# A transformer layer on one core: softmax sums from the blocks of maxima in place of a product with ones

## The reference

```
x = x + 0.5 * ffn(layernorm(x))      # ffn: weights rounded to -1, 0, 1 times their mean size, plus bias
x = x + attention(layernorm(x))
x = x + 0.5 * ffn(layernorm(x))

# attention: 16 heads of 32; b = 4, s = 1024
kqv = x @ Wqkv + bqkv
scores[k, q] = k_row . q_row / sqrt(32)     # kept where k <= q (triu), else -10000
attn = softmax(scores, over k)              # the kept ones of each q sum to 1
out = (attn^T @ v) @ Wo + bo
```

## Time and profile before

| | us |
|---|---|
| median of 3 runs | 1316.94 (1316.63 to 1317.14) |
| the profiled execution | 1315.88 |
| its span | 1313.7 |
| PE, DVE, ACT, POOL busy | 1235.4, 832.7, 501.9, 348.2 |
| L1079, the product with ones, PE | 160.3 |
| L747 and L741, maxima, DVE | 220.4 and 159.0 |
| L758, reciprocals, DVE | 118.9 |
| L897, exponentials, ACT | 314.6 |

### The profile page before, as it was taken

How to read it: one execution, slowest core, us unless ns; L and a number is a source line. 1 busy time by engine, 2 the same in 40 slices (tenths; PEclk the granted TensorE clock), 3 DMA queues, 4 the chain that set the end, 5 groups by cost and what they waited for, 6 DMA issues and landing times.

```text
span 1313.7 us, 27193 instructions
## 1 busy us (share of the span) xinstructions
PE 1235.4 (94%) x10938; PEld 749.1 (57%) x10938; DVE 832.7 (63%) x2048; ACT 501.9 (38%) x1139; POOL 348.2 (27%) x492
## 2 busy tenths in 40 slices
PE   4689999999999999999999999999999999998886
PEld 3466554555666565655656565655656566654454
DVE  6764556688545667689645767679644666655444
ACT  1222434344434334343433434344443434334421
POOL 4821110245001222236100322336201222300233
PEclk8898999999999999999999999999999999989988
DMA  7422201011103001321102102311102102000110
GB/s 240 145 81 80 83 34 59 26 63 44 42 2 130 18 34 49 114 82 49 50 1 99 49 10 74 113 66 58 41 18 73 58 26 74 26 10 10 42 49 32
DMA packets 40685, 77.26 MB, mean 59 GB/s; under 512 B 5232, under 2 KB 10352, under 8 KB 40560
## 3 DMA queue, kind: packets, MB, share of 16 engines
q1 hardware_dynamic: 40560, 75.52, 17.0%
HBM read 49.81 MB, written 25.17 MB: 57 GB/s over the span
## 4 chain that ended last, share of the span: by engine, by line
PE 84%; DVE 9%; issue 3%; POOL 2%; ACT 2%; DMA 1%; SPq 0%; DVEq 0%; ACTq 0%; POOLq 0%
PE bank L964 28%; PE bank L1024 11%; PE bank L1046 11%; PE bank L1068 10%; PE bank L1079 9%; PE bank L989 8%; PE bank L981 3%; PE bank L1052 3%; DVE mst L741 2%; DVE st L701 1%; DVE hn L712 1%; ACT prob L897 1%; DVE junk L747 1%; DVE xt L732 1%; POOL rstd L617 1%
## 5 line engine op out<-in xcount | busy, mean ns | idle before, releaser
L897 ACT ACTIVATE prob<-bank 128x512 f32<-128x512 f32 (+3 forms) x768 | 314.6, 497 | 311.2 <-PE bank L1052 310.7
L747 DVE CUSTOM_DVE_ANT_0 junk<-bank,mask 128x384 bf16<-128x384 f32 (+3 forms) x512 | 220.4, 487 | 144.4 <-PE bank L1024 143.8
L741 DVE TENSOR_REDUCE mst<-bank 128x1 f32<-128x512 f32 x256 | 159.0, 684 | 121.0 <-PE bank L1024 121.0
L1046 PE MATMUL bank<-qT,kT 32*128 32x512 f32 (+2 forms) x2304 | 190.8, 384 | 11.2 <-DVE mst L741 5.9
L652 POOL TENSOR_SCALAR_AFFINE_SELECT prob<-prob 128x512 f32<-128x512 f32 x128 | 81.3, 635 | 446.2 <-ACT prob L897 446.1
L964 PE MATMUL bank<-hT,wqk 128*128 128x512 f32 x768 | 194.4, 402 | 0.0
L1024 PE MATMUL bank<-kT,qT 32*128 32x512 f32 (+2 forms) x2304 | 182.1, 383 | 4.2 <-DVE mst L741 1.7
L1024 PEld LDWEIGHTS bank<-kT,qT 32*128 32x128 f32 x2304 | 103.0, 184 | 135.7 <-issue 94.8
L964 PEld LDWEIGHTS bank<-hT,wqk 128*128 128x128 f32 x768 | 141.1, 190 | 38.3 <-issue 7.6
L1079 PE MATMUL bank<-prob,ones 128*32 128x512 f32 (+3 forms) x1536 | 160.3, 489 | 0.0
L1046 PEld LDWEIGHTS bank<-qT,kT 32*128 32x128 f32 x2304 | 105.8, 184 | 93.6 <-issue 45.6
(11 more groups left out here) (76 smaller groups left out, 1096.4 us busy)
## 6 DMA issues: line engine op xcount, KB each, us to landing
wqk<-weight_scratch SPq DMA_DIRECT2D x30, 512.0 KB, 3.3
wvo<-weight_scratch SPq DMA_DIRECT2D x20, 512.0 KB, 6.0
xt<-in_L_attn_x_dram SPq DMA_DIRECT2D x32, 256.0 KB, 3.7
residual_scratch<-xt SPq DMA_DIRECT2D x32, 256.0 KB, 2.0
xt<-residual_scratch SPq DMA_DIRECT2D x32, 256.0 KB, 3.6
out_dram<-xt SPq DMA_DIRECT2D x32, 256.0 KB, 2.0
o<-in_L_attn_Wqkv_dram SPq DMA_DIRECT2D x12, 256.0 KB, 4.6
weight_scratch<-o SPq DMA_DIRECT2D x6, 512.0 KB, 3.0
```

What stands on the lines that cost most here:

```text
L741: nc.vector.tensor_reduce(mst[:, 1, at:at + 1], psum(u, h), AX, ALU.max).then_inc(ring_free, 1)
L747: nc.vector.tensor_tensor_reduce(junk[:, turn % 2, 0:n], psum(u, h)[:, 0:n], mask[:, CW - n:CW], 1.0, -3e38, ALU.add, ALU.max, mst[:, 2 * ...
L897: nc.scalar.activation(prob[:, at % 2, h, off:CW], psum(("S", b, n), h)[:, off:CW], ACT.Exp, scale=SCALE)\
L1046: nc.tensor.matmul(psum(u, h)[:, off:CW], kT[g % 2][row, x, P * kb:P * kb + P], qT[g % 2][row, y, CW * c + off:CW * c + CW], start=(term = ...
```

## The change

`sums`, its bank and the copy of it go. Bank 6 joins the ring, which has now 7 banks; the values are gathered in bank 7. The maxima are taken in one form for all blocks, which also writes the scaled, negated and masked block back to its bank in PSUM and keeps the smallest value, so that `mst` holds -SCALE times the maximum. ACT then takes the exponential of the block in its bank, with that column as bias, and adds along the row into a column of `ssum`. A bank of an A block is free when ACT has done that (`a_free`). For chunk 1, whose two blocks of keys have maxima of their own, the two sums are joined with the exponentials of the differences (`msh`). DVE inverts 16 columns at once; a unit "N" turns them round, splits them and brings them by two transfers to `rall`, 8 rows; a unit "C" spreads them over the partitions by one product with `pick`, and DVE multiplies the values with it. The text rows name C and N, and some O, T3, F2 and V move by a step or two. On ACT and in the numbering of splits, M and N come ahead of the T, and the sums of an A block lie between them and the T.

```
-RING = 6
+RING = 7
...
 GROUP2_ROWS = (
-    "P | A | X1.0",
-    "P | A | X1.1",
+    "C P | A | X1.0",
+    "N P | A | X1.1",
     "M P | A | X1.2",
-    "F2.7 T1.0 P | A | X1.3",
-    "T1.1 F1.0 | A | X1.4",
+    "T1.0 P | A | X1.3",
+    "C T1.1 F1.0 | A | X1.4",
     "T1.2 F1.1 | A | X1.5",
-    "T2.0 T1.3 F1.2 | A | X1.6",
+    "N T2.0 T1.3 F1.2 | A | X1.6",
...
             def maximum(u):
...
+                n, off = (CW, 0) if kc < c else (P * (r + 1), CW - P * r)
                 for h in range(4):
                     at = 4 * h + r
-                    if kc < c:
-                        nc.vector.tensor_reduce(mst[:, 1, at:at + 1], psum(u, h), AX, ALU.max).then_inc(ring_free, 1)
-                        continue
...
-                    nc.vector.tensor_tensor_reduce(junk[:, turn % 2, 0:n], psum(u, h)[:, 0:n], mask[:, CW - n:CW],
-                                                   1.0, -3e38, ALU.add, ALU.max, mst[:, 2 * c, at:at + 1])\
-                        .then_inc(ring_free, 1)
+                    nc.vector.tensor_tensor_reduce(psum(u, h)[:, 0:n], psum(u, h)[:, 0:n], mask[:, off:off + n],
+                                                   -SCALE, BIG, ALU.add, ALU.min, mst[:, c + kc, at:at + 1])\
+                        .then_inc(a_max, 1)
...
+            def inverse(u):
+                _, b, g, c = u
+                at = group(b, g)
+                if c == 0:
+                    dve.wait_ge(a_free, block_at(maxima(b, g, 0)[-1]))
+                    of = ssum[:, 0, :]
+                else:
+                    dve.wait_ge(shift_exp, at)
+                    nc.vector.tensor_tensor(msh[:, :, :], msh[:, :, :], ssum[:, 1:3, :], ALU.mult)...
+                    nc.vector.tensor_tensor(msh[:, 0, :], msh[:, 0, :], msh[:, 1, :], ALU.add)...
+                    of = msh[:, 0, :]
...
+                nc.vector.reciprocal(rcol[:, :], of).then_inc(inverse_done, 1)
+
+            def scaled(u):
...
+                dve.wait_ge(ring_full, full(u))
+                of = chunk(b, CHUNKS * g + c)
+                nc.vector.tensor_tensor(of, psum(u), of, ALU.mult).then_inc(ring_free, 1)
...
+            def block_sums(u):
...
+                for h in range(4):
+                    at = 4 * h + r
+                    act.wait_ge(a_max, block_at(u, h))
+                    nc.scalar.activation(psum(u, h)[:, 0:n], psum(u, h)[:, 0:n], ACT.Exp, bias=mst[:, c + kc, at:at + 1],
+                                         scale=-1.0, accum_out=ssum[:, c + kc, at:at + 1]).then_inc(a_free, 1)
+                if u == maxima(b, g, 1)[-1]:
+                    act.wait_ge(shift_done, group(b, g))
+                    nc.scalar.activation(msh[:, :, :], msh[:, :, :], ACT.Exp, scale=-1.0).then_inc(shift_exp, 1)
...
         # ACT, in each step
                 for u in s.uses():
-                    if u[0] in ("T1", "T2", "T3", "M"):
+                    if u[0] in ("M", "N"):
+                        high(u)
+                    elif u[0] == "C":
+                        evacuate(u)
+                for u in s.uses():
+                    if u[0] == "A":
+                        block_sums(u)
+                for u in s.uses():
+                    if u[0] in ("T1", "T2", "T3"):
                         high(u)
...
         # PE
+                elif kind == "C":
+                    pe.wait_ge(pick_set, 3)
+                    pe.wait_ge(rall_in, 32 * (ended(u) + 1))
+                    nc.tensor.matmul(psum(u), pick[:, :], rall[:, :], start=True, stop=True).then_inc(ring_full, 1)
...
-            def sums(b, n):
...
-                for h in range(4):
-                    m = nc.tensor.matmul(accs[HD * h:HD * h + HD, off:CW], ones[:, 0:HD], prob[:, at % 2, h, off:CW],
-                                         start=(kb == 0), stop=(kb == QPC * (c + 1) - 1))
```

More of the change, by code:

```diff
@@ L293, in use @@
             self.full[u] = full
-            if u[0] != "V":
+            if u[0] not in ("A", "V"):
                 self.freed[u] = freed
@@ L339, in macaron_kernel @@
         onesr = sb("onesr", [P, P], F32R)
+        pick = sb("pick", [8, P], F32R)
         hb = sb("hb", [P, D])
@@ L429, in split_tile, with ended, before @@
             return hts[HAT[u] % 2]
+        def ended(u):
+            return (group(u[1], u[2]) - 1) * CHUNKS + u[3]
+        def before(b, g):
+            return (b, g - 1) if g else (b - 1, GROUPS - 1)
         def chunk(b, n):
@@ L538, in rows, with inverse_rows @@
                         .then_inc(mrow_in[c], 16)
+            def inverse_rows(u):
+                _, b, g, c = u
+                sp.wait_ge(ring_free, freed(u))
+                if ended(u):
+                    sp.wait_ge(ring_full, full(("C", b, g, c - 1) if c else ("C", *before(b, g), 1)))
+                for part in (HI, LO):
+                    sp.dma_start(rall[4 * part:4 * part + 4, :].bitcast(F32), rrow[:, part, :].bitcast(F32))\
+                        .then_inc(rall_in, 16)
             def load(w):
@@ L602, in _ @@
             pool.wait_ge(set_pool, 7)
+            nc.gpsimd.memset(pick[:, :].bitcast(F32), 0.0).then_inc(pick_set, 1)
+            for part in (HI, LO):
+                pool.wait_ge(pick_set, part + 1)
+                to = pick[:, :].rearrange("p (h n) -> p h n", h=4)
+                nc.gpsimd.affine_select(out=to, in_=to.bitcast(F32), compare_op=ALU.not_equal, fill=1.0, base=-4 * part,
+                                        pattern=[[-1, 4], [0, HD]], channel_multiplier=1).then_inc(pick_set, 1)
+            pool.wait_ge(pick_set, 3)
             pool.wait_ge(set_b, 48)
@@ new lines, in maximum @@
+                if u == maxima(b, g, 1)[-1]:
+                    dve.wait_ge(a_max, block_at(u))
+                    nc.vector.tensor_tensor(mcol[:, :], mst[:, 1, :], mst[:, 2, :], ALU.min).then_inc(mcol_done, 1)
+                    dve.wait_ge(mcol_done, group(b, g))
+                    for n in range(2):
+                        i = nc.vector.tensor_tensor(msh[:, n, :], mst[:, 1 + n, :], mcol[:, :], ALU.subtract)
+                    i.then_inc(shift_done, 1)
+            def inverse(u):
+                _, b, g, c = u
+                at = group(b, g)
[4 more added lines that the diff above has]
+                    dve.wait_ge(shift_exp, at)
+                    nc.vector.tensor_tensor(msh[:, :, :], msh[:, :, :], ssum[:, 1:3, :], ALU.mult).then_inc(inverse_done, 1)
+                    dve.wait_ge(inverse_done, 4 * at - 2)
+                    nc.vector.tensor_tensor(msh[:, 0, :], msh[:, 0, :], msh[:, 1, :], ALU.add).then_inc(inverse_done, 1)
+                    dve.wait_ge(inverse_done, 4 * at - 1)
+                    of = msh[:, 0, :]
+                if ended(u):
+                    dve.wait_ge(ring_full, full(("N", b, g, c - 1) if c else ("N", *before(b, g), 1)))
+                nc.vector.reciprocal(rcol[:, :], of).then_inc(inverse_done, 1)
@@ L775, in use @@
                     c = u[3]
-                    low(u, mrow[:, c, LO, :], psum(u)[0:4 * QPC, 0:P], mrow[:, c, HI, :], (-1.0, ALU.mult))
+                    low(u, mrow[:, c, LO, :], psum(u)[0:4 * QPC, 0:P], mrow[:, c, HI, :], (1.0 / SCALE, ALU.mult))
+                elif kind == "N":
+                    low(u, rrow[:, LO, :], psum(u)[0:4 * QPC, 0:P], rrow[:, HI, :])
+                elif kind == "C":
+                    scaled(u)
                 elif kind == "T2":
@@ L784, in use @@
                     residual(u, {"F1": 0, "O": 1, "F2": 2}[kind])
[L786 to L799, removed]
             for k, s in enumerate(SLOTS):
@@ L836, in high @@
                 elif kind == "M":
[L837 removed]
+                    i = nc.scalar.activation(mrow[:, u[3], HI, :], psum(u)[0:4 * QPC, 0:P], ACT.Identity, scale=1.0 / SCALE)
+                elif kind == "N":
+                    if ended(u):
+                        act.wait_ge(rall_in, 32 * ended(u))
+                    i = nc.scalar.activation(rrow[:, HI, :], psum(u)[0:4 * QPC, 0:P], ACT.Identity)
                 elif kind == "T2":
@@ L1092, in _ @@
                     values(*done)
-                    sums(*done)
                 for u in s.uses():
```

191 lines of the change are left out of this document (85 added, 106 removed).

## The result

The changed kernel takes 1302.5 us (median of 4, 1299.1 to 1304.4) against 1317.0 before: a ratio of 0.9885, 95% interval 0.9863 to 0.9906. It is faster by 14.5 us, where 32 were forecast. The time lies inside the stated range, the size is less than half of the forecast.

A forecast was written before the change was run, and what follows sets the result against it. PE was taken to bound second and fourth groups, DVE the last eight steps of third ones, neither the bare groups. Group gains and losses, block sums and the end summed to -32 us, giving 1285 us, range 1238 to 1330.

The forecast's parts named there:

- the two bare groups ... -1 each; the first and the last group together -1: Second group of batch 0, third of batch 3, and the end groups: PE has slack, ACT room, so little gain.
- I leave it there: PE's granted clock, 0.95 to 1.00 in the stretches read, was taken as unchanged by the change.
- PE's release: Product with ones goes, C and N come: net 6.8 us a group, 109 us in all; fourth groups gain 5.1 each.
- every piece taken from PE is time: Second and fourth groups, PE busy 72.44 of 72.50 and 75.06 of 75.11 us: removed PE work shortens them.
- The seventh bank: Ring of 7 for 6 loosens S and A by one bank; credited only against the slower release by ACT.
- The price on ACT: 768 exponentials with sums on ACT, 0.72 us each at 512 columns, 470 us in all; ACT busy about 952 us.
- rival 1: ACT bound in every full-width step: sums at 0.80 us cancel the gain, at 0.85 the time is 1342; chance 0.25.
- The hidden wait: DVE stands 1.6 to 1.75 us each T step for ACT's high half; third groups of three batches +3.5 us each.
- Second groups: Second groups of three batches: half of DVE's 1.9 us excess counted, gain 4.2 us each, -12.6 in all.
- The end: Last outputs: reciprocals replaced by one matmul and a product, tail's normalisations one row earlier: -6 us.
- DVE's write to PSUM: Full-width maxima written to PSUM: taken as no extra cost, ends -0.03 and +0.10 us each over 768.
- the four: ACT bound, 1342 us (0.25); cheap sum, 1249 (0.22); everything hidden, PE alone counts, 1211 (0.08); all cancels, 1317 (0.03).

The follow-up runs named there:

- The fillers: Changed kernel with four idle PE products ahead of the scores in 25 steps whose step before holds no P, O, V or F: 1271.3 us, ratio 0.9634.
- with ACT's columns and both losses out of the way: Changed kernel with four idle products in 25 steps, T's high halves ahead of the block sums, and block sums over 8 columns only: 1203.8 us, ratio 0.9143.
- few-ones kernel: Kernel before the change with the product with ones made only in a chunk's first step, 32 in place of 192: 1276.0 us, ratio 0.9681.
- reordered kernel: Changed kernel with only ACT's order altered, high halves of T1, T2 and T3 ahead of the block sums: 1278.4 us, ratio 0.9699.
- both edits: Changed kernel with four idle PE products in 25 steps and ACT's high halves of T ahead of the block sums: 1244.7 us, ratio 0.943.

## Why the prediction was wrong

**The step that failed** is the line of the sum "the two bare groups ... -1 each; the first and the last group together -1", and with it the sentence "I leave it there" on the clock. I had compared ACT's 53 us with the 61 to 65 of the group and found room. But PE has slack there, and the change both takes work from PE and makes it stand longer, for DVE and ACT in turn. The clock went to its lower level for much of these groups (means 0.73, 0.74 and 0.77), and the term measured +22.6 where -3 stood. The fillers show it: at a clock of 0.97 to 1.00 the same groups take 62.1, 59.7 and 51.8 us. Without this step the forecast sum would have been near: the other terms forecast -29 and measured -36 us of span. That they agree so well is in part luck: the second groups missed by 6.4 us one way and the end by 6.8 the other.

**PE's release.** The release forecast for full groups holds up: fourth ones fell by 5.6 to 6.1, with 5.1 forecast, and with ACT's columns and both losses out of the way by 7.4, for 6.8 of net release. What was wrong is the reason, that there "every piece taken from PE is time". With six banks the few-ones kernel gains only 4 of 6.0 us in a fourth group. The seventh bank, to which the prediction gave no value of its own, is worth 78 us to the changed kernel; that it would give the few-ones kernel the missing 2 us was not tried.

**The price on ACT.** 0.67 us measured for 0.72 (bounds 0.56 and 0.89). That is a right mechanism with a slightly high size. Columns cost 41 us in all with the clock held, in the manner of rival 1 but far from its deciding point of 0.80.

**The hidden wait.** It came out as forecast in place: third groups +11.4 us for +10.5, DVE's waits for high halves 89.1 us for 13.0 before. A timeline of DVE in a third group answers to the earlier trace rows, where hT follows with no gap:

```profile
888.98 0.27 DVE L751 SCALAR_TENSOR_TENSOR mrow<-bank,mrow 16x128 fp32r<-16x128 f32 x1
890.44 0.69 DVE L749 TENSOR_TENSOR hT<-bank,hT 128x512 fp32r<-128x512 f32 x1 [1.19 <-ACT hT L878]
891.05 0.68 DVE L749 TENSOR_TENSOR hts<-bank,hts 128x512 fp32r<-128x512 f32 x1
```

It is 1.19 us here, behind a narrow block and 0.27 us of M's row, for 1.6 forecast; over all 65 waits the mean is 1.4 us. The close size of the third groups is in part luck, since some of the 11.4 us is clock: with the fillers alone, ACT's order as it was, the third group of batch 0 takes 83.6 us at 0.96 for 87.3 at 0.92. That ACT's order is the cause was argued from the code and is shown by the reordered kernel, 24 us less.

**Second groups** gained 6.2 of 12.6 us: I let light steps catch up half of DVE's excess, and they caught up less; with the order mended they gain 12.7. **The end** gained 12.8 for 6: it lost the inversions, and one row of normalisation goes ahead. The clock there is 0.95 for 0.87 before, which is some 3 us of it: with both edits, at 0.88, the end takes 43.8 us for 40.8. What gave the rest was not tried. **DVE's write to PSUM** costs 724 ns for 687 and starts every 0.65 us for about 0.61: small, inside its bounds. The Trainium skill's higher cost for DVE in PSUM ("Perfetto Trace Analysis", Optimizing Scalar/DVE Operations) points the right way; 37 ns is what this case shows of its 65, with the input in PSUM in both forms. For ACT, 0.66 us in PSUM with a bias against 0.69 into SBUF goes its way too, though it is another function.

**Rivals.** Of the four none happened as told. Rival 1 had the right sign of the miss by the wrong cause.

## What to carry to other kernels

Before work is taken off TensorE, look group by group at where it already stands. There the removed work may have been what kept its clock up, and the stands that a change adds take it down further; a busy time that falls less than the removed work is the sign, and a few idle products in the stand are a cheap test and, here, a gain of 31 us. Where a unit is added to an in-order engine, ask which unit behind it another engine waits for; putting that one first gave 24 us for three moved lines. And when an engine is added to the readers of a bank, count what a bank more or less is worth.

## What the runs showed of the hardware

- An addition along the row on ACT is an instruction of its own of 206 ns, of which about 0.1 us, by the estimate above, adds to the distance from one start to the next; a 512-column exponential with it goes every 0.67 us, one without (immediate bias, into SBUF) every 0.52.
- PE's granted clock fell to means of 0.74 and 0.73 in two groups in which PE stands in the steps without P (0.6 to 1.5 us in one piece in those read, 2.3 where a few products lie in between), though its rows cover 63.32 of 71.54 us: at the low level the rows themselves are longer, 1.87 us for 0.99. The busy share alone does not show it.
- Four idle products in a step's stand held the clock at 0.97 and 1.00 in these groups. With one it was 0.73 in the one and 0.94 in the other.
